# Encoder convolution net on two images: the order in which the level 1 matmul groups of the two images are issued

## The chip, the cores and the metric
One core of one Trainium2 chip runs the program once per launch. The metric is the device time of that launch in microseconds; the profile is of one such execution, and its times count from the first instruction of the span.

## The reference
`x` is (2 images, 32 channels, 64, 64), float32. Each channel is normalized over its plane, then a small U-shaped net runs, and its result is added to `x`. `BN_S` is a constant near 1.

```python
def basic_block(x, w1, w2, stride=1, ds=None):
    out = jax.nn.relu(conv3(x, w1, stride) * BN_S)
    out = conv3(out, w2, 1) * BN_S
    identity = conv1x1(x, ds, stride) * BN_S if ds is not None else x
    return jax.nn.relu(out + identity)
x = basic_block(x, e0b0c1, e0b0c2)
x = basic_block(x, e0b1c1, e0b1c2)
f0 = x
x = basic_block(x, e1b0c1, e1b0c2, stride=2, ds=e1b0ds)     # level 1
x = basic_block(x, e1b1c1, e1b1c2)
f1 = x
x = basic_block(x, e2b0c1, e2b0c2, stride=2, ds=e2b0ds)     # level 2
x = basic_block(x, e2b1c1, e2b1c2)
x = (jax.nn.relu(deconv2(x, dec0w) * BN_S) + f1) * BN_S
x = (jax.nn.relu(deconv2(x, dec1w) * BN_S) + f0) * BN_S
```

## The kernel before
Everything stays in SBUF between the input load and the output stores. A map is held as 2 x 2 pixel blocks: the 128 partitions are 4 pixel positions times 32 channels. A 3 x 3 convolution then is a few shifted matmuls from partitions to partitions.

Level 0 and level 1 work in "pieces": one image, a range of block rows, one PSUM bank. Level 1 has four stages, called here by their Python names: `down` (weights e1b0c1, stride 2), `block` (e1b0c2 and the shortcut e1b0ds), `odd` (e1b1c1) and `last_1` (e1b1c2). Each stage has two pieces per image, an upper and a lower one ("turned", its partition halves exchanged); such a pair goes together. The two pairs of a stage take four of the eight banks, so `down` and `odd` share banks 0 to 3, `block` and `last_1` share banks 4 to 7.

All matmuls of these pieces are 64 x 64 quarters of the array. Of a pair, the long products (`mains`: four shifts per piece, six in `down`) use one pairing of quarters and the short ones (`minors`: two shifts, three in `down`) the other, into the same bank; so `minors` first waits on the semaphore `mains_done` until the last of its pair's `mains` has ended. In the trace a float32 matmul shows as two records: `mains` of a pair are 32 records (48 in `down`), `minors` 16 (24 in `down`).

- `free_banks(pair)` makes TensorE (PE) wait until the pieces that held the pair's banks before are evacuated. For `down` and `block` these are the eight pieces of e0b1c2, the last stage of level 0: `down[0]` and `down[1]` wait for the four of image 0, `block[0]` for the first two of image 1 and `block[1]` for its last two.
- `mains` waits for its weights and for the pair's source: `down` for the stride planes `planes1` of its image (`wait_planes`; written by ACT L537 and L635 and by DVE L738 and L741 from `block0`, which DVE L791 adds up piece by piece), every other stage for both pieces of its image in the stage before.
- `shortcut_products(block[i])` (L1035, 16 records) reads `planes1` and starts the bank of `block[i]`; `identity_products(last_1[1])` (L1045, 8 records) reads `flat1` and starts the bank of `last_1[1]`. The `mains` of those pairs wait until they have ended.

The sums leave PSUM in the order of the pieces, which DVE and ACT have written out by hand: DVE takes both pieces of a `down` or `odd` pair (L783); of a `block` pair DVE takes the upper (L799) and ACT the lower (L558). Of `last_1`, image 0's two pieces go over DVE (L805 adds `flat1` to the sums), then DVE and ACT each make `planes2` of one (L748, L570) and gather `sides2` from it (DVE L758 in `gather(0)`, ACT L588 in `gather_sides(0)`). Image 1's follow behind that on both engines: DVE L748 and ACT L570 straight from PSUM, then sides and the corners (L762, L581).

Level 2 handles both images in one matmul. Its first stage, e2b0c1, runs `of_image(0)` (L1123, 4 records) once `planes2` of image 0 is there, then three whole products (L845, 6 records) after `even_planes` shows that both engines have made the first planes of both images, then `of_image(1)`, then the products of `sides2`. From there on each stage needs the whole result of the stage before.

ACT also rearranges the skip data of level 0 (L550, `gather_skip0`) between its level 1 evacuations, and GpSimd adds it up (L477).

Of the kernel before, what the change touches and what calls it, by code (L numbers as in the profile page):

```python
# [157 lines left out]
def previous_in_bank(piece):  # L158

    return max((p.index for p in PIECES[:piece.index] if bank_index(p.index) == bank_index(piece.index)), default=None)  # L160
# [21 lines left out]
def build(nc, x, consts, weights, out):  # L182
    ctx = ExitStack()
    with ctx:
# [3 lines left out]
        def sem(name):  # L188
            return ctx.enter_context(nc.semaphore(name))
# [26 lines left out]
        inside = [sb(f"inside{v}", [P, 1, SLOTS[v] * PITCH[v]]) for v in (0, 1)] + [sb("inside2", [P, IMAGES, RUN[2]])]  # L216
        zeros = sb("zeros", [P, BANK // 2], BF16)
        raw = sb("raw", [P, RAW_SLOTS, max(m for _, m, _ in WEIGHTS), P])
        w_sb = [sb(f"w_{n}", [P, 1, 9, P]) if n == "e1b0c1" else sb(f"w_{n}", [P, 1, m, P]) for n, m, _ in WEIGHTS]
        turned = {n: sb(f"turned_{n}", [P, 9 if n == "e1b0c1" else 4, P])  # L220
# [29 lines left out]
        mains_done = sem("mains_done")  # L250
# [24 lines left out]
        def wait_w(engine, k):  # L275

            if k == 0:
                engine.wait_ge(w_loaded[0], 16)
            else:
                engine.wait_ge(w_hi, k)  # L280
# [7 lines left out]
        def turned_rows(piece):  # L288

            return piece.row >= BLOCKS[STAGES[piece.stage].level] // 2  # L290
# [21 lines left out]
        def flat1_inside(piece):  # L312

            first = (piece.row + 1) * PITCH[1] + 1
            lines = flat1[:, piece.images[0], first:first + piece.rows * PITCH[1]]
            return lines.rearrange("p (r c) -> p r c", c=PITCH[1])[:, :, 0:BLOCKS[1]]
# [31 lines left out]
        def wait_evacuated(engine, index):  # L348

            wait_for(engine, index, evacuated_by)  # L350

        def of_stage(name, image):

            return [p for p in PIECES if p.stage == STAGE[name] and image in p.images]
# [9 lines left out]
        def sums_of(piece):  # L364

            stage, pitch = STAGES[piece.stage], PITCH[STAGES[piece.stage].level]
            if stage.level == 2:
                run = (EVEN_RUN if stage.kind == "even" else RUN)[2]
                return bank_of(piece)[:, 0:IMAGES * run].rearrange("p (i n) -> p i n", i=IMAGES)
            columns = BLOCKS[stage.level] if stage.kind == "even" else pitch  # L370
            return bank_of(piece)[:, 0:piece.rows * columns].rearrange("p (r c) -> p r c", c=columns)
# [45 lines left out]
        block = ctx.enter_context(nc.Block())  # L417
# [421 lines left out]
        def _(pe):  # L839
# [26 lines left out]
            def wait_source(piece):  # L866

                image, last = piece.images[0], last_row_read(piece)
                if piece.stage == 0:
                    pe.wait_ge(norm_by_dve, 2 * image + (1 if last < sum(NORM_BY_DVE[0]) else 2))  # L870
                    if last >= NORM_BY_ACT[0]:
                        pe.wait_ge(norm_by_act, image + 1)
                elif STAGES[piece.stage].kind == "down":
                    wait_planes(pe, 1, image)
                elif STAGES[piece.stage].level == 0:
                    wait_made(pe, last_piece(piece.stage - 1, piece.images, last))
                else:
                    for of_rows in [p for p in PIECES if p.stage == piece.stage - 1 and p.images[0] == image]:
                        wait_made(pe, of_rows.index)
# [97 lines left out]
            def mark(instruction):  # L977

                instruction.then_inc(mains_done, 1)
                marks[0] += 1  # L980
                return marks[0]

            def free_banks(pair):

                for piece in pair:
                    if previous_in_bank(piece) is not None:
                        wait_evacuated(pe, previous_in_bank(piece))

            def mains(pair, first=True, count=4, between=None):

                wait_w(pe, W_INDEX[STAGES[pair[0].stage].name])
                for piece in pair:
                    wait_source(piece)
                product = down_product if STAGES[pair[0].stage].kind == "down" else tile_product
                for n in range(count):
                    for piece in pair:
                        last = product(piece, True, n, first=(first and n == 0))
                    if n == 1 and between is not None:
                        between()
                return mark(last)  # L1000

            def minors(pair, done, count=2):

                pe.wait_ge(mains_done, done)
                product = down_product if STAGES[pair[0].stage].kind == "down" else tile_product
                for n in range(count):
                    for piece in pair:
                        last = product(piece, False, n, final=(n == count - 1))
                        if n == count - 1:
                            last.then_inc(summed, 1)  # L1010
# [12 lines left out]
            def shortcut_products(pair):  # L1023

                wait_w(pe, W_INDEX["e1b0ds"])
                for p in range(2):
                    for piece in pair:
                        h = int(turned_rows(piece))
                        first = (piece.row + 1 + 2 * h) * PITCH[1] + 1
                        of_h = slice(HALF * h, HALF * h + HALF)  # L1030
                        for c in range(2):
                            of_c = slice(HALF * c, HALF * c + HALF)
                            lines = planes1[of_h, piece.images[0], c, p, first:first + piece.rows * PITCH[1]].rearrange(
                                "p (r c) -> p r c", c=PITCH[1])[:, :, 0:BLOCKS[1]]
                            last = pe.matmul(sums_of(piece)[of_c], shortcut1[of_h, p], lines, start=(p == 0), stop=False,  # L1035
                                             skip_group_check=True)
                return mark(last)

            def identity_products(pair):

                pe.wait_ge(eye_loaded, 16)
                for piece in reversed(pair):
                    for c in range(2):
                        of_c = slice(HALF * c, HALF * c + HALF)
                        last = pe.matmul(sums_of(piece)[of_c], eye[of_c, of_c], flat1_inside(piece)[of_c], start=True,  # L1045
                                         stop=False, skip_group_check=True)
                return mark(last)
# [6 lines left out]
            for first in range(0, len(LEVEL0), GROUP):  # L1054
# [3 lines left out]
            pe.wait_ge(zeros_set, 6)  # L1058
            down, block, odd, last_1 = [[of_stage(name, image) for image in range(IMAGES)]
                                        for name in ("e1b0c1", "e1b0c2", "e1b1c1", "e1b1c2")]  # L1060
            free_banks(down[0])
            down_0 = mains(down[0], count=6)
            free_banks(block[0])
            shortcut_0 = shortcut_products(block[0])
            minors(down[0], down_0, count=3)
            free_banks(down[1])
            down_1 = mains(down[1], count=6)
            pe.wait_ge(mains_done, shortcut_0)
            block_0 = mains(block[0], first=False)
            minors(down[1], down_1, count=3)  # L1070
            free_banks(block[1])
            shortcut_1 = shortcut_products(block[1])
            minors(block[0], block_0)
            pe.wait_ge(mains_done, shortcut_1)
            block_1 = mains(block[1], first=False)
            free_banks(odd[0])
            odd_0 = mains(odd[0])
            minors(block[1], block_1)
            minors(odd[0], odd_0)
            free_banks(odd[1])  # L1080
            odd_1 = mains(odd[1])
            free_banks(last_1[0])
            last_0 = mains(last_1[0])
            minors(odd[1], odd_1)
            minors(last_1[0], last_0)
            free_banks(last_1[1])
            identity = identity_products(last_1[1])
            pe.wait_ge(mains_done, identity)
            minors(last_1[1], mains(last_1[1], first=False))

            def sums_2(name):

# [183 lines left out]
```

## Time and profile before

| | us |
|---|---|
| runs shown | 84.66, 85.80, 85.91 (median 85.8) |
| the profiled execution | 84.97 |
| its span, first to last instruction | 83.1 |
| level 1, first `down` matmul to first level 2 matmul | 51.99 to 67.77 |
| PE busy, share of the span | 74.2, 89% |
| DVE busy; ACT busy | 34.5; 43.1 |

A timeline row reads: start, length, engine, line, operation, output <- input, size, count; in brackets the idle time of the engine before it and what ended it. A merged row covers its count of instructions, in which the engine may have overlapped others; a matmul's shown length contains its way through the array, so groups of matmuls are measured from start to start.

### The profile page before, as it was taken

What the parts mean: (1) busy time and instruction counts of PE and PEld (TensorE: products, weight loads), DVE (VectorE), ACT (ScalarE), POOL (GpSimd) and SP (SyncE); (2) the same over time, 40 slices, a digit from 0 to 9 for tenths busy, and PEclk for the clock granted to TensorE, in tenths of its full rate; (3) what the DMA queues carried; (4) which work ended last, traced back from release to release, by engine and by line L of the source; (5) the groups of instructions that cost most, each with busy time, mean ns of one, the idle gap of its engine ahead of it and who ended that gap; (6) DMA issues with size and microseconds to landing.
All of it is one profiled execution on the core that took longest, in us unless ns stands there. A gap on an engine that the chain in (4) does not pass through costs nothing.

```text
span 83.1 us, 3230 instructions
## 1 busy us (share of the span) xinstructions
PE 74.2 (89%) x1395; PEld 60.9 (73%) x1395; DVE 34.5 (42%) x137; ACT 43.1 (52%) x113; POOL 8.5 (10%) x26
## 2 busy tenths in 40 slices
PE   4957799999999999999999999999999999799700
PEld 3735686777888887777788888999889878686500
DVE  5459829505736051070250742830412557113630
ACT  6006008980008999999757590997129367002300
POOL 7400000000000000000000009100650000000330
PEclk9999999999999999999999999999999999999999
DMA  1857990064000000409583000000000000000094
GB/s 13 237 167 197 326 351 10 0 166 122 8 0 8 0 0 8 130 10 317 179 270 114 8 0 0 8 0 8 0 8 0 8 0 0 0 0 0 8 323 182
DMA packets 4190, 6.62 MB, mean 80 GB/s; under 512 B 465, under 2 KB 2129, under 8 KB 4177
## 3 DMA queue, kind: packets, MB, share of 16 engines
q1 hardware_dynamic: 4032, 6.29, 23.8%
q8 instruction: 11, 0.18, 0.9%
q10 hardware_dynamic: 144, 0.13, 0.5%
q14 instruction: 3, 0.02, 0.1%
HBM read 5.37 MB, written 1.05 MB: 77 GB/s over the span
## 4 chain that ended last, share of the span: by engine, by line
PE 82%; DVE 6%; DMA 4%; issue 2%; SPq 1%; DVEq 0%
PE psum L955 63%; PE psum L845 7%; PE psum L970 6%; DMA x_sb<-x_in 4%; DVE late_a L834 2%; DVE late_b L701 1%; PE psum L1123 1%; PE psum L1035 1%; SPq L424 1%; PE psum L920 1%; PE psum L1170 1%; DVE stats L672 1%; DVE moments L685 1%; PE psum L913 1%; PE psum L887 1%
## 5 line engine op out<-in xcount | busy, mean ns | idle before, releaser
L955 PE MATMUL psum<-late_b,w_e0b0c 64*64 64x264 f32 (+1 forms) x192 | 11.5, 393 | 1.0 <-DVE late_b L701 1.0
L955 PE MATMUL psum<-late_b,w_e0b1c 64*64 64x264 f32 (+1 forms) x192 | 11.3, 391 | 0.0
L783 DVE SCALAR_TENSOR_TENSOR late_a<-psum,inside 128x297 f32<-128x297 f32 (+1 forms) x16 | 6.4, 444 | 11.8 <-PE psum L955 11.6
L955 PEld LDWEIGHTS psum<-late_b,w_e0b0c 64*64 64x64 f32 x192 | 8.2, 132 | 3.8 <-issue 1.5
L955 PE MATMUL psum<-late_a,w_e0b0c 64*64 64x256 f32 x96 | 10.6, 376 | 0.0
L955 PE MATMUL psum<-late_a,w_e0b1c 64*64 64x256 f32 x96 | 10.6, 375 | 0.0
L955 PE MATMUL psum<-late_a,turned_e0b0c 64*64 64x256 f32 x96 | 10.5, 375 | 0.0
L955 PE MATMUL psum<-late_a,turned_e0b1c 64*64 64x256 f32 x96 | 10.5, 375 | 0.0
L955 PEld LDWEIGHTS psum<-late_b,w_e0b1c 64*64 64x64 f32 x192 | 8.4, 132 | 2.7
L477 POOL TENSOR_TENSOR normed<-normed,x_sb 128x1024 f32<-128x1024 f32 x2 | 4.7, 2360 | 53.7 <-ACT normed L577 46.9
L955 PEld LDWEIGHTS psum<-late_a,w_e0b0c 64*64 64x64 f32 x96 | 7.7, 132 | 1.2
L955 PEld LDWEIGHTS psum<-late_a,w_e0b1c 64*64 64x64 f32 x96 | 7.7, 132 | 1.1
L955 PEld LDWEIGHTS psum<-late_a,turned_e0b1c 64*64 64x64 f32 x96 | 7.3, 132 | 0.5
L955 PEld LDWEIGHTS psum<-late_a,turned_e0b0c 64*64 64x64 f32 x96 | 7.3, 132 | 0.6
L904 PE MATMUL psum<-zeros 128*128 128x256 bf16 x37 | 6.5, 335 | 1.1 <-DVE eps L706 1.1
L621 ACT ACTIVATE late_b<-block 128x256 f32<-128x256 f32 x8 | 2.8, 412 | 6.9 <-DVE block L788 6.8
L904 PEld LDWEIGHTS psum<-zeros 128*128 128x128 bf16 x37 | 4.3, 120 | 2.3 <-DVE eps L706 1.1
L791 DVE SCALAR_TENSOR_TENSOR block<-block,psum 128x256 f32<-128x256 f32 x8 | 3.0, 418 | 6.2 <-PE psum L955 6.0
L550 ACT ACTIVATE late_b<-normed 128x128 f32<-128x128 f32 x16 | 5.4, 434 | 0.0
L970 PE MATMUL psum<-planes,w_e1b0c 64*64 64x153 f32 x72 | 5.3, 289 | 0.0
L970 PE MATMUL psum<-planes,turned_e1b0c 64*64 64x153 f32 x72 | 5.2, 289 | 0.0
L595 ACT ACTIVATE scratch<-moments,eps 128x1 f32<-128x1 f32 x2 | 0.6, 295 | 8.7 <-DVE moments L685 8.7
(134 smaller groups left out, 131.9 us busy)
## 6 DMA issues: line engine op xcount, KB each, us to landing
x_sb<-x_in SPq DMA_DIRECT2D x4, 160.0 KB, 3.3
raw<-e0b1c_in SPq DMA_DIRECT2D x2, 256.0 KB, 4.2
raw<-e1b1c_in SPq DMA_DIRECT2D x2, 256.0 KB, 2.9
raw<-e2b1c_in SPq DMA_DIRECT2D x2, 256.0 KB, 2.8
raw<-e1b0c_in SPq DMA_DIRECT2D x1, 448.0 KB, 5.3
raw<-e2b0c_in SPq DMA_DIRECT2D x1, 448.0 KB, 3.2
x_sb<-x_in SPq DMA_DIRECT2D x2, 192.0 KB, 3.1
out<-late_a SPq DMA_DIRECT2D x1, 384.0 KB, 2.9
```

The source lines that it names most:

```text
L424: sp.dma_start(x_sb[:, image, row:row + rows, :], x[:, image, row:row + rows, :]).then_inc(x_loaded[image][n], 16)
L477: pool.tensor_tensor(normed[:, image], normed[:, image], x_sb[:, image], ALU.add).then_inc(skip0_added, 1)
L550: last = act.activation(target, source, ACT.Copy)
L621: act.activation(flat_inside(image, piece.row, piece.rows), block0_of(piece), ACT.Relu).then_inc(hi_ready, 1)
L672: last = dve.bn_stats(stats[:, image, STATS * n:STATS * (n + 1)], x_sb[:, image, row:row + rows, :])
L783: dve.scalar_tensor_tensor(out=odd_of(piece), in0=sums, scalar=0.0, in1=mask_of(piece), op0=ALU.max, op1=ALU.mult).then_inc(relu_ready, 1)
L791: dve.scalar_tensor_tensor(out=block0_of(piece), in0=block0_of(piece), scalar=0.0, in1=sums, op0=ALU.max, op1=ALU.add).then_inc(relu_ready, 1)
L834: dve.scalar_tensor_tensor(out=result[:, n], in0=last_bank(n), scalar=0.0, in1=skip0_of(n), op0=ALU.max, op1=ALU.add).then_inc(result_read ...
L845: last = pe.matmul(within(target, columns), w, within(moving, columns), start=(first and n == 0), stop=(final and n == len(terms) - 1), sk ...
L904: pe.matmul(psum[:, bank, 0:256], zeros[:, 0:P], zeros[:, 0:256], start=True, stop=True)
L955: last = pe.matmul(target, weights_of, moving, start=first, stop=final, skip_group_check=True)
L970: last = pe.matmul(bank_of(piece)[of_c, 0:count], w[of_h, 3 * s + t, HALF * o:HALF * o + HALF], planes1[of_h, piece.images[0], s % 2, t % ...
```

## The change
The calls at the head of `pe`'s level 1 are put in another order; no instruction of level 1 is added or dropped. Written as m (`mains`), n (`minors`), s (`shortcut_products`), i (`identity_products`), with the stage's letter (d, b, o, l) and the image:

```
before: d0m s0 d0n d1m b0m d1n s1 b0n b1m o0m b1n o0n o1m l0m o1n l0n i1 l1m l1n
after:  d0m s0 d1m d0n s1 d1n b0m b1m b0n b1n o0m o1m o0n o1n l0m i1 l1m l0n l1n
```

`free_banks` of `down[1]` and of `block[0]` stand ahead of everything. DVE's, ACT's and GpSimd's programs are the same.

```diff
-            free_banks(down[0])
+            for pair in down:
+                free_banks(pair)
+            free_banks(block[0])
             down_0 = mains(down[0], count=6)
-            free_banks(block[0])
             shortcut_0 = shortcut_products(block[0])
+            down_1 = mains(down[1], count=6)
             minors(down[0], down_0, count=3)
-            free_banks(down[1])
-            down_1 = mains(down[1], count=6)
+            free_banks(block[1])
+            shortcut_1 = shortcut_products(block[1])
+            minors(down[1], down_1, count=3)
             pe.wait_ge(mains_done, shortcut_0)
             block_0 = mains(block[0], first=False)
-            minors(down[1], down_1, count=3)
-            free_banks(block[1])
-            shortcut_1 = shortcut_products(block[1])
-            minors(block[0], block_0)
             pe.wait_ge(mains_done, shortcut_1)
             block_1 = mains(block[1], first=False)
-            free_banks(odd[0])
-            odd_0 = mains(odd[0])
+            minors(block[0], block_0)
             minors(block[1], block_1)
-            minors(odd[0], odd_0)
-            free_banks(odd[1])
-            odd_1 = mains(odd[1])
-            free_banks(last_1[0])
-            last_0 = mains(last_1[0])
-            minors(odd[1], odd_1)
-            minors(last_1[0], last_0)
-            free_banks(last_1[1])
-            identity = identity_products(last_1[1])
-            pe.wait_ge(mains_done, identity)
-            minors(last_1[1], mains(last_1[1], first=False))
+            for stage in (odd, last_1):
+                first = []
+                for pair in stage:
+                    free_banks(pair)
+                    added = identity_products(pair) if pair is last_1[1] else None
+                    if added is not None:
+                        pe.wait_ge(mains_done, added)
+                    first.append(mains(pair, first=added is None))
+                for pair, main in zip(stage, first):
+                    minors(pair, main)
```

## Rows read from the trace of the kernel before

**Rows 1.** The page's row of the granted TensorE clock in 40 slices.
```profile
PEclk9999999999999999999999999999999999999999
```

**Rows 2.** Chain that ended last, level 1: start, length, piece of work.
```profile
52.21 1.56 PE psum L970 x48
53.77 0.44 PE psum L1035 x16
...
57.42 0.78 PE psum L970 x24
```

**Rows 3.** Timeline of PE, level 1.
```profile
51.99 0.29 PE L970 MATMUL psum<-planes,turned_e1b0c 64*64 64x153 f32 x1
...
61.03 0.30 PE L955 MATMUL psum<-odd,turned_e1b0c 64*64 64x128 f32 x2
...
61.47 0.73 PE L955 MATMUL psum<-flat,w_e1b1c 64*64 64x153 f32 x16
62.42 1.22 PE L955 MATMUL psum<-flat,w_e1b1c 64*64 64x153 f32 x32 [0.22 <-issue]
63.42 0.30 PE L955 MATMUL psum<-odd,w_e1b1c 64*64 64x128 f32 x2
...
64.30 0.73 PE L955 MATMUL psum<-flat,w_e1b1c 64*64 64x153 f32 x16
64.82 0.30 PE L955 MATMUL psum<-odd,turned_e1b1c 64*64 64x128 f32 x2
...
65.26 0.64 PE L1045 MATMUL psum<-flat,eye 64*64 64x128 f32 x8
65.98 0.33 PE L955 MATMUL psum<-odd,w_e1b1c 64*64 64x128 f32 x2
...
67.17 0.33 PE L955 MATMUL psum<-odd,w_e1b1c 64*64 64x128 f32 x2
```

**Rows 4.** Timeline of DVE, end of level 0 to the start of level 2.
```profile
51.38 1.62 DVE L791 SCALAR_TENSOR_TENSOR block<-block,psum 128x256 f32<-128x256 f32 x4 [2.46 <-PE psum L955]
...
53.92 0.18 DVE L741 TENSOR_SCALAR planes<-block 128x32 f32<-128x32 f32 x1
...
58.24 0.54 DVE L783 SCALAR_TENSOR_TENSOR odd<-psum,inside 128x153 f32<-128x153 f32 x2 [2.68 <-PE psum L970]
...
61.72 0.29 DVE L799 TENSOR_SCALAR flat<-psum 128x128 f32<-128x128 f32 x1 [2.31 <-PE psum L955]
...
65.54 0.47 DVE L805 TENSOR_TENSOR with_identity<-flat,psum 128x128 f32<-128x128 f32 x2
...
66.57 0.62 DVE L758 COPY sides<-planes 32x82 f32<-32x82 f32 x3 [0.34 <-ACT planes L570]
```

**Rows 5.** Timeline of ACT, level 1 to level 2.
```profile
61.78 0.28 ACT L558 ACTIVATE flat<-psum 128x128 f32<-128x128 f32 x1 [2.33 <-PE psum L955]
...
66.05 0.42 ACT L570 ACTIVATE planes<-with_identity 128x64 f32<-128x64 f32 x2 [1.38 <-DVE with_identity L805]
66.56 0.83 ACT L588 ACTIVATE sides<-planes 64x82 f32<-64x82 f32 x3
67.93 0.34 ACT L570 ACTIVATE planes<-psum 128x64 f32<-128x64 f32 x2 [0.54 <-PE psum L955]
```

**Rows 6.** Timeline of PE's weight loads (PEld), which start a group after a wait.
```profile
59.11 0.17 PEld L955 LDWEIGHTS psum<-odd,w_e1b0c 64*64 64x64 f32 x2 [0.28 <-issue]
...
67.77 0.52 PEld L1123 LDWEIGHTS psum<-planes,w_e2b0c 128*128 128x128 f32 x4 [0.17 <-issue]
68.21 0.79 PEld L845 LDWEIGHTS psum<-planes,w_e2b0c 128*128 128x128 f32 x6
```

**Rows 7.** Timeline of PE at the start of the kernel.
```profile
1.07 3.75 PE L904 MATMUL psum<-zeros 128*128 128x256 bf16 x18 [1.07 <-DVE eps L706]
5.77 0.41 PE L887 MATMUL psum<-stats,same_channel 32*128 32x18 f32 x8 [0.94 <-DVE stats L672]
6.12 1.70 PE L904 MATMUL psum<-zeros 128*128 128x256 bf16 x14
```

## The prediction
> **What bounds the kernel now.** I read the page first, then the chain that ended last, then the timelines of PE, DVE and ACT side by side from the end of level 0 to the first stage of level 2. PE is busy for 89% of the span and the granted clock is at full speed throughout [rows 1]; the chain through level 1 is almost all PE [rows 2]. So in level 1 the time is the length of PE's instruction list plus the gaps in it, and a new order of the same instructions can only win or lose gaps. Behind level 1 the bound changes: level 2 needs both images, and its stages hang on DVE and ACT in turn. So I need three things from the rows: how long each group takes start to start, how long PE must wait from the end of one pair's short products to the next stage's long ones of that image (the turn), and how much work of DVE and ACT is hidden today because image 0 is ahead.
>
> **Lengths of the groups.** d-mains 1.56, shortcuts 0.44, d-minors 0.78 us [rows 2]. o-mains 63.42 - 62.42 = 1.00; l-mains 64.30 - 63.42 = 0.88, and b-mains, of the same 32 records and size, 0.88 too; o-minors 64.82 - 64.30 = 0.52; b-minors 61.47 - 61.03 = 0.44, l-minors likewise; identity with the wait for its end 65.98 - 65.26 = 0.72 [rows 3].
>
> **The turn.** For `down` and `odd`, where DVE takes both pieces: b1m's weights start at 59.11 [rows 6], 0.33 behind DVE's end at 58.24 + 0.54 = 58.78 [rows 4], and its first matmul about 0.03 later, at 59.14. d1n, whose sums those are, was issued to 57.99: b1m comes after s1 (0.44) and b0n (0.44) and an idle time of 0.28 before 59.14 [rows 2, 6]. Turn: 59.14 - 57.99 = 1.15 us. For `block`, where DVE and ACT share: b1n was issued to 61.47, ACT ended at 61.78 + 0.28 = 62.06 [rows 5], o1m started at 62.42 [rows 3]. Turn: 0.95 us. Whatever PE has to do between the two counts as cover; the rest is a gap.
>
> **Gaps in level 1 before.** b1m 0.28 [rows 6]. o1m: cover o0n, 0.52 of 0.95, gap 0.43. l1m: 0.72 with the identity products, of which 8 records at 27 ns (0.44 over 16, rows 2 say) would be 0.22; the rest is the wait for them. l1n: it waits for its own long products with nothing between, 67.17 - 65.98 - 0.88 = 0.31 gap [rows 3].
>
> **Part 1, the head.** d0m starts at 51.99 now, right behind level 0 [rows 3]. In the new order PE first waits for `block[0]`'s banks, the first two of DVE's four evacuations that start at 51.38 and take 1.62 together [rows 4]; the second ends at about 51.38 + 0.81 = 52.19. With the 0.36 from a releaser's end to the first matmul (as at b1m and o1m) d0m starts at 52.5, a gap of 0.5. Queued behind it is all of level 1. Then d0m and s0 run to 54.5. d1m now follows at once and needs image 1's planes, which DVE finishes at 53.92 + 0.18 = 54.10 [rows 4]; plus 0.36 is 54.46. So the two new waits lie over each other: without the first the second would cost 0.46. Bounds for both: 0.4 to 0.6; I take 0.5. Moving `free_banks(down[1])` costs nothing, since its banks were emptied before 51.38; the cover that d0n gave d1m is what is gone.
>
> **Part 2, the middle.** d1m ends at 56.09 (54.53 + 1.56), d0n 56.87, s1 57.31, d1n 58.09. b0m needs 56.87 + 1.15 = 58.02: just covered, by 0.07. b0m to 58.97. b1m needs 58.09 + 1.15 = 59.24: gap 0.27, as before. b1m to 60.12, b0n 60.56, b1n 61.00. o0m needs 60.56 + 0.95 = 61.51: its only cover is b1n, **a new gap of 0.51**. o0m to 62.51, o1m 63.51 (covered by o0m; the old gap of 0.43 is gone), o0n 64.03, o1n 64.55. l0m needs 64.03 + 1.15 = 65.18: its only cover is o1n, **a new gap of 0.63**. l0m to 66.06, identity and its wait to 66.78 (as before, nothing between them), l1m to 67.66, l0n 68.10 and l1n from 68.10 (the old gap of 0.31 is covered by l0n). Against 67.17 that is +0.93. As a sum of gaps: 0.50 + 0.51 + 0.63 - 0.43 - 0.31 = +0.90, and 0.03 rounding.
>
> **Part 3, the passage to level 2.** Before, l0n was issued to 65.26, and i1, l1m and l1n hid image 0's evacuation; only image 1's stood behind l1n. Now l0n ends at 68.10, and both engines do image 0's share in front of image 1's. L805 started 0.28 after l0n [rows 3, 4] although DVE had L783 to do just ahead; 0.25 is the usual step (61.47 to 61.72). So L805 starts at 68.35. From the start of L805, ACT's L570 started 0.51 and its L588 ended at 66.56 + 0.83 = 67.39, that is 1.85 later [rows 4, 5]; DVE's L758 ended at 67.19, 1.65 later [rows 4]. In the new order DVE is free for image 1 at 70.0 and ACT at 70.2. l1n's sums have been waiting there since 68.8. ACT's L570 for image 1 then starts at 70.25 in place of 67.93 [rows 5], 2.3 later. `even_planes` releases the three whole products (L845), which started loading at 68.21 [rows 6]: now at 70.5. `of_image(0)` takes 0.44 [rows 6] and runs from 69.6, in the shade. All that follows, sides, corners and the rest of level 2 and the decoder, hangs on the same two engines' image 1 work and moves by the same 2.3. Of that, 0.93 is PE's delay and 1.4 is image 0's evacuation, uncovered. Bounds of the second: nothing if DVE and ACT could have done image 0's share under l1n entirely (they can't: L805 alone needs l0n, which ends 0.44 before l1n does), and 1.85 - 0.44 + 0.3 = 1.7 if every wait falls on the bad side. GpSimd's second L477 and ACT's second `gather_skip0` move by 0.1 us with d1n and end near 64.3, long before L805 at 68.35: hidden.
>
> **Sum.** +0.93 + 1.37 = +2.3 us. Against the profiled execution: 84.97 + 2.3 = 87.3 (span 83.1 to 85.4). The median of the runs shown is 0.8 above that execution, by which it would be 88.1. The four times before lie at 84.7 and 85.0 or at 85.8 and 85.9, so I put the forecast between: 87.7.
>
> **A rule weighed.** New idle times of PE are 0.5, 0.5, 0.6 in level 1 and, from l1n's last matmul at 68.8 to 69.6, 0.8, then 0.4. At the start of the kernel PE was idle for 0.94 before 5.77, and the 14 warm-up matmuls right behind took 1.70 together, (1.70 - 0.33)/13 = 0.105 each, that is at full speed; the first 18 took 3.75, 0.20 each [rows 7]. So an idle time of that length left the clock up. The Trainium skill, "TensorE: Matmul & The Clock Gate", section "Why this matters for your kernels", warns that the array falls back to its lower clock when PE sits idle between bursts for too long. By it the new pauses could halve the clock of level 2, which is the third rival below; this trace gives it little weight.
>
> **Rivals.** (1) *Less is uncovered in the passage.* If image 1's work on DVE and ACT is not what level 2's start hangs on, or image 0's overlaps more of l1n, only PE's 0.93 and a part of the 1.4 remain: +0.9 to +1.6, 86.2 to 86.9 by the middle of the times. Against it: the chain in the code is serial on each engine. (2) *Faster: the pairs cover each other.* The two removed gaps (o1m, l1n) give 0.74, b1m's could go too. If the turn were no longer than the other image's short products, 0.44 to 0.52, the new gaps at o0m and l0m would vanish, and 84.6 would follow if also the passage were hidden by l1n. It decides at a turn of about 0.5; the rows show 0.95 and 1.15 for the very same instructions. (3) *The clock falls in level 2.* From 69.6 PE's share of the rest is some 8 us; at the warm-up's two rates, 0.20 to 0.105, that adds up to 7 us: 95. (4) *Nothing changes*, because PE reorders or hid it: against it, groups start in the order of the code in every row.
>
> **How the numbers follow.** Forecast 75%, rival 1 15%, rival 2 3%, rival 3 3%, rival 4 4%. The forecast's own spread is the two clusters of times (+-0.6) with 0.4 of the sum. Range 86.5 to 88.9: it takes in the upper part of rival 1 and leaves out the others. A measurement of this kernel can tell about 2% from no change, 1.7 us; my 2.3 is 2.7%, not far above it. Slower by over 2%: 0.76; within: 0.20; faster: 0.04.
>
> **What would show it.** In the changed profile: d0m's first record near 52.5; L955 with idle times of about 0.5 before o0m and 0.6 before l0m, none before l1n; l1n from 68.1; DVE L805 at 68.3; ACT's L588 of image 0 ending near 70.2; L845 on planes at 70.5; the last stores 2.3 later. The prediction is wrong if L845 comes clearly before 70, if the turns are shorter than 0.95 when both images are in step, or if PEclk falls.

## The result

The changed kernel runs in 88.06 us (median of 4; 87.26 to 88.30) against 85.34 us (84.66 to 85.91) for the kernel before: ratio 1.035, 95% interval 1.029 to 1.041, slower by about 2.7 us at the medians. The times of either kernel lie in two groups (before: 84.66 and 84.89, or 85.80 and 85.91), the upper of which comes from the start of the kernel, as the next rows show. The changed kernel's profiled execution took 88.16 us, the span 86.3 us, 3.2 more than before. PE is busy for 77.0 us in place of 74.2, again 89% of the span.

Of these 3.2 us 0.74 are not of the change: they arise at the start, where both kernels are the same. The timeline of PE at the start of the changed kernel:

```profile
1.07 4.02 PE L904 MATMUL psum<-zeros 128*128 128x256 bf16 x18 [1.07 <-DVE eps L706]
5.47 0.63 PE L887 MATMUL psum<-stats,same_channel 32*128 32x18 f32 x8 [0.38 <-DVE stats L672]
6.03 3.17 PE L904 MATMUL psum<-zeros 128*128 128x256 bf16 x14
9.13 1.13 PE L955 MATMUL psum<-late_b,w_e0b0c 64*64 64x297 f32 x8
```

The 14 warm-up matmuls took 3.17 us; in the profile of before 1.70 [rows 7]. From start to start that is (3.17 - 0.42)/13 = 0.21 us each, with 0.42 the shown length of one, against 0.105 before: half the speed, 1.2 in place of 2.4 GHz. The clock records in the two traces agree: the granted clock is recorded at full speed from 9.99 us on in the changed kernel, from 4.42 us on before. Level 0 then starts 0.33 later (9.13; before it was 8.80, from the timeline) and needs 0.41 longer to its last matmul row, since 9.13 to 9.99 ran at half speed. To keep this out, I measure each profile from the last matmul row of level 0 (51.82 before, from the timeline; 52.56 in the changed kernel): level 1 and all behind it lost 3.2 - 0.74 = 2.5 us.

Timeline of the changed kernel, PE with its weight loads, end of level 0 to level 2:

```profile
52.56 0.39 PE L955 MATMUL psum<-late_a,w_e0b1c 64*64 64x256 f32 x2
53.55 0.17 PEld L970 LDWEIGHTS psum<-planes,w_e1b0c 64*64 64x64 f32 x2 [1.06 <-issue]
53.58 0.35 PE L970 MATMUL psum<-planes,w_e1b0c 64*64 64x153 f32 x2 [0.63 <-DVE block L791]
...
62.03 0.27 PE L955 MATMUL psum<-odd,w_e1b0c 64*64 64x128 f32 x2
62.61 0.36 PE L955 MATMUL psum<-flat,w_e1b1c 64*64 64x153 f32 x4 [0.31 <-ACT flat L558]
...
66.28 0.33 PE L955 MATMUL psum<-odd,w_e1b1c 64*64 64x128 f32 x2 [0.43 <-DVE odd L783]
...
67.18 0.63 PE L1045 MATMUL psum<-flat,eye 64*64 64x128 f32 x8
67.87 0.33 PE L955 MATMUL psum<-odd,w_e1b1c 64*64 64x128 f32 x2
...
69.23 0.27 PE L955 MATMUL psum<-odd,turned_e1b1c 64*64 64x128 f32 x1
...
69.57 0.28 PE L955 MATMUL psum<-odd,w_e1b1c 64*64 64x128 f32 x2
...
70.50 0.52 PEld L1120 LDWEIGHTS psum<-planes,w_e2b0c 128*128 128x128 f32 x4 [0.89 <-DVE planes L748]
71.47 0.67 PEld L845 LDWEIGHTS psum<-planes,w_e2b0c 128*128 128x128 f32 x5 [0.45 <-ACT planes L570]
```

Three waits are new: d0m at 53.58 waits for DVE's L791 (before it followed level 0 at once, [rows 3]); o0m at 62.61 waits for ACT's L558; l0m at 66.28 for DVE's L783. Behind l1n, which now follows l0n at once (from 69.23), level 2 waits twice, for L748 and for L570. The same stretch on DVE and ACT, to be held against [rows 4, 5]:

```profile
52.12 1.62 DVE L791 SCALAR_TENSOR_TENSOR block<-block,psum 128x256 f32<-128x256 f32 x4 [2.46 <-PE psum L955]
...
65.38 1.06 DVE L783 SCALAR_TENSOR_TENSOR odd<-psum,inside 128x153 f32<-128x153 f32 x4 [2.73 <-PE psum L955]
69.46 0.48 DVE L805 TENSOR_TENSOR with_identity<-flat,psum 128x128 f32<-128x128 f32 x2 [3.02 <-PE psum L955]
...
69.97 0.41 ACT L570 ACTIVATE planes<-with_identity 128x64 f32<-128x64 f32 x2 [4.67 <-DVE with_identity L805]
70.48 0.83 ACT L588 ACTIVATE sides<-planes 64x82 f32<-64x82 f32 x3
71.22 0.30 ACT L570 ACTIVATE planes<-psum 128x64 f32<-128x64 f32 x2
```

DVE sees the sums of both `odd` pairs as one run of four, and L805 starts 3.9 us later than before (69.46 against 65.54), ACT's second L570 3.3 us later (71.22 against 67.93), with the 0.74 of the start in both.

### The profile page after: what moved, and what is told of

It is laid out like the page before. It is cut to its first block, busy times and chain, and to the rows that moved or that the text cites. A ratio compares the mean times of both kernels' runs of the same rounds, so it can differ in the third digit from the quotient of the medians.

```text
span 86.3 us, 3230 instructions
## 1 busy us (share of the span) xinstructions
PE 77.0 (89%) x1395; PEld 61.2 (71%) x1395; DVE 34.5 (40%) x137; ACT 43.0 (50%) x113; POOL 8.6 (10%) x26
## 4 chain that ended last, share of the span: by engine, by line
PE 82%; DVE 6%; DMA 4%; issue 2%; ACT 2%; DVEq 0%; ACTq 0%
PE psum L955 60%; PE psum L845 7%; PE psum L970 6%; PE psum L904 4%; DMA x_sb<-x_in 4%; DVE late_a L834 2%; DVE stats L672 2%; PE psum L1035 1%; DVE odd L783 1%; ACT sides L588 1%; PE psum L920 1%; PE psum L887 1%; ACT planes L570 1%; PE psum L1167 1%; DVE with_identity L805 1%
## 5 line engine op out<-in xcount | busy, mean ns | idle before, releaser
L783 DVE SCALAR_TENSOR_TENSOR late_a<-psum,inside 128x297 f32<-128x297 f32 (+1 forms) x16 | 6.4, 445 | 11.7 <-PE psum L955 11.6
L955 PEld LDWEIGHTS psum<-late_b,w_e0b0c 64*64 64x64 f32 x192 | 7.6, 137 | 3.9 <-issue 1.1
L904 PE MATMUL psum<-zeros 128*128 128x256 bf16 x37 | 8.2, 399 | 1.1 <-DVE eps L706 1.1
L904 PEld LDWEIGHTS psum<-zeros 128*128 128x128 bf16 x37 | 5.0, 139 | 2.9 <-DVE eps L706 1.1
L791 DVE SCALAR_TENSOR_TENSOR block<-block,psum 128x256 f32<-128x256 f32 x8 | 3.0, 418 | 6.2 <-PE psum L955 6.0
L970 PEld LDWEIGHTS psum<-planes,w_e1b0c 64*64 64x64 f32 x72 | 4.7, 132 | 1.1 <-issue 1.1
```

What stands on the lines that cost most here:

```text
L783: dve.scalar_tensor_tensor(out=odd_of(piece), in0=sums, scalar=0.0, in1=mask_of(piece), op0=ALU.max, op1=ALU.mult).then_inc(relu_ready, 1)
L791: dve.scalar_tensor_tensor(out=block0_of(piece), in0=block0_of(piece), scalar=0.0, in1=sums, op0=ALU.max, op1=ALU.add).then_inc(relu_ready, 1)
L904: pe.matmul(psum[:, bank, 0:256], zeros[:, 0:P], zeros[:, 0:256], start=True, stop=True)
L955: last = pe.matmul(target, weights_of, moving, start=first, stop=final, skip_group_check=True)
L970: last = pe.matmul(bank_of(piece)[of_c, 0:count], w[of_h, 3 * s + t, HALF * o:HALF * o + HALF], planes1[of_h, piece.images[0], s % 2, t % ...
```

## The experiments

One number is read from each profile, called **D** here: the start of the weights of level 2's whole products (PEld L845 on `planes`) less the start of the last matmul row of level 0. It is free of what happens at the start, and behind it all twelve profiles take nearly the same time to the end of the span (14.8 to 15.1 us). The kernel before has 68.21 - 51.82 = 16.39; the changed one 71.47 - 52.56 = 18.91, which is +2.52. The table gives D less 16.39 and the measured ratio to the kernel before. D is read from one execution of each kernel; the intervals of the ratios are 0.4 to 0.8 us to either side, wider than most steps between neighbours, so the steps rest on D and the times only agree with them.

| kernel | D less 16.39, us | ratio, 95% interval |
|---|---|---|
| the change | +2.52 | 1.035 (1.029 to 1.041) |
| late_frees | +2.14 | 1.021 (1.014 to 1.029) |
| l0n_early | +2.28 | 1.023 (1.015 to 1.032) |
| both_parts | +1.65 | 1.014 (1.008 to 1.020) |
| after_single | +1.70 | 1.016 (1.010 to 1.022) |
| l0n_last | +1.43 | 1.019 (1.009 to 1.028) |
| early_frees | +0.85 | 1.010 (1.006 to 1.015) |
| single_waits | -0.39 | 0.998 (0.993 to 1.002) |
| fewer_waits | -0.45 | 0.995 (0.990 to 0.999) |
| early_identity | -0.46 | 0.992 (0.988 to 0.997) |
| warm_21 | -0.46 | 0.990 (0.984 to 0.995) |

### late_frees: the hoisted waits put back

```diff
-            for pair in down:
-                free_banks(pair)
-            free_banks(block[0])
+            free_banks(down[0])
             down_0 = mains(down[0], count=6)
+            free_banks(block[0])
             shortcut_0 = shortcut_products(block[0])
+            free_banks(down[1])
             down_1 = mains(down[1], count=6)
```

> The changed kernel, but the waits for free banks of block[0] and down[1] stand behind d0m again, as before the change. In the changed profile d0m starts 0.87 us behind level 0 (corrected for a start of the kernel that took 0.74 longer), where I had forecast 0.5. Theory: that whole gap comes from the hoisted waits (DVE's second evacuation, then a row of waits that PE passes one by one). Then d0m follows level 0 without a gap, and d1m waits for image 1's planes in its place, to about 2.5 us behind d0m's start in place of 2.0; L845 on planes comes 0.35 us earlier than in the changed kernel measured from level 0's end, and the time is +2.1 us against before (ratio 1.025) where the changed kernel has +2.5 in its profile. Rival: the gap is image 1's planes or something else at the head, and nothing moves (+2.5).

PE and its weight loads in this kernel:

```profile
51.81 0.39 PE L955 MATMUL psum<-late_a,w_e0b1c 64*64 64x256 f32 x2
51.99 0.29 PE L970 MATMUL psum<-planes,turned_e1b0c 64*64 64x153 f32 x1
...
54.42 0.17 PEld L970 LDWEIGHTS psum<-planes,w_e1b0c 64*64 64x64 f32 x2 [0.47 <-issue]
...
70.34 0.67 PEld L845 LDWEIGHTS psum<-planes,w_e2b0c 128*128 128x128 f32 x5 [0.45 <-ACT planes L570]
```

d0m follows level 0 at once, and d1m waits in its place, 0.47 on the weight loads, for image 1's planes. D falls by 0.38 (0.35 expected): the hoisted waits cost the change 0.38, not the whole 0.85 that d0m lost (53.58 - 52.56 = 1.02, where 51.99 - 51.82 = 0.17 before).

### early_frees: only the hoisted waits, in the kernel before

```diff
-            free_banks(down[0])
+            for pair in down:
+                free_banks(pair)
+            free_banks(block[0])
             down_0 = mains(down[0], count=6)
-            free_banks(block[0])
             shortcut_0 = shortcut_products(block[0])
             minors(down[0], down_0, count=3)
-            free_banks(down[1])
             down_1 = mains(down[1], count=6)
```

> The kernel before, and of the change only the waits for free banks of down[1] and block[0] ahead of d0m. Theory (the hoisted wait and the wait of d1m for image 1's planes lie over each other in the change, which is why late_frees gave back only 0.37): here d1m comes behind d0n and never waits for planes, so the whole delay of d0m, 0.9 to 1.0 us, goes to the end: ratio 1.011. Rival: a delay at the head costs 0.4 wherever it stands: ratio 1.004.

```profile
52.98 0.39 PE L955 MATMUL psum<-late_a,w_e0b1c 64*64 64x256 f32 x2
53.98 0.35 PE L970 MATMUL psum<-planes,w_e1b0c 64*64 64x153 f32 x2 [0.61 <-DVE block L791]
...
70.22 0.67 PEld L845 LDWEIGHTS psum<-planes,w_e2b0c 128*128 128x128 f32 x5
```

D is +0.85: here the whole delay of d0m (53.98 - 52.98 = 1.00, less 0.17) reaches the end. The same three lines cost 0.85 or 0.38, by what stands behind them; in the change they lie over the planes wait of d1m. I had said 0.9 to 1.0 and the ratio 1.011; measured 1.010.

### l0n_last and l0n_early: one pair of short products, moved both ways

In the kernel before, l0n behind l1m (l0n_last):

```diff
             minors(odd[1], odd_1)
-            minors(last_1[0], last_0)
             free_banks(last_1[1])
             identity = identity_products(last_1[1])
             pe.wait_ge(mains_done, identity)
-            minors(last_1[1], mains(last_1[1], first=False))
+            last_1_main = mains(last_1[1], first=False)
+            minors(last_1[0], last_0)
+            minors(last_1[1], last_1_main)
```

> The kernel before, with one pair of short products, l0n, moved behind l1m, as the change has it; all else as before. Theory: l1m starts as before, since it waits for DVE's evacuation of o1n anyhow, l1n starts only 0.13 later (its own gap of 0.31 is covered by l0n's 0.44), but image 0's evacuation begins 2.0 us later and stands in front of image 1's: L845 on planes at about 69.6 in place of 68.2, time +1.35 us (ratio 1.016), which is the part of the change's loss behind PE. Rival: the passage hangs on l1n only: +0.1 us (ratio 1.001).

In the changed kernel, l0n ahead of i1 and l1m again (l0n_early):

```diff
                     free_banks(pair)
+                    if pair is last_1[1]:
+                        minors(last_1[0], first[0])
                     added = identity_products(pair) if pair is last_1[1] else None
...
                 for pair, main in zip(stage, first):
-                    minors(pair, main)
+                    if pair is not last_1[0]:
+                        minors(pair, main)
```

> The changed kernel, with the one pair of short products l0n moved back ahead of i1 and l1m. Theory (image 0's evacuation of last_1, 1.8 us on ACT, stands uncovered behind l0n): PE itself loses 0.3 at l0n and 0.3 at l1n, which now wait for their own long products, but image 0's evacuation is over when l1n ends, so L845 on planes comes 0.6 us EARLIER than in the changed kernel, time about +1.8 us against before. Rival (level 2's start follows PE's last product, and the evacuation of image 0 is a side matter): 0.6 LATER, +3.1 us.

The passage in l0n_last, on PE, DVE, ACT and the weight loads:

```profile
51.49 0.39 PE L955 MATMUL psum<-late_a,w_e0b1c 64*64 64x256 f32 x2
...
67.29 0.48 DVE L805 TENSOR_TENSOR with_identity<-flat,psum 128x128 f32<-128x128 f32 x2 [1.95 <-PE psum L955]
...
68.31 0.83 ACT L588 ACTIVATE sides<-planes 64x82 f32<-64x82 f32 x3
69.06 0.30 ACT L570 ACTIVATE planes<-psum 128x64 f32<-128x64 f32 x2
...
69.31 0.67 PEld L845 LDWEIGHTS psum<-planes,w_e2b0c 128*128 128x128 f32 x5 [0.45 <-ACT planes L570]
```

One move of 16 records costs 1.43 us, where I had said 1.35: L805 starts 67.29 - 51.49 = 15.80 behind level 0, before it was 65.54 - 51.82 = 13.72, and ACT comes to image 1's L570 only after image 0's L588; L845 is released by it. The rival (+0.1) is out. The other way round, in the changed kernel:

```profile
52.33 0.39 PE L955 MATMUL psum<-late_a,w_e0b1c 64*64 64x256 f32 x2
...
67.27 0.46 PEld L955 LDWEIGHTS psum<-odd,w_e1b1c 64*64 64x64 f32 x3 [0.38 <-issue]
67.61 0.14 PEld L955 LDWEIGHTS psum<-odd,turned_e1b1c 64*64 64x64 f32 x2
...
70.56 0.52 PEld L1123 LDWEIGHTS psum<-planes,w_e2b0c 128*128 128x128 f32 x4 [0.17 <-issue]
71.00 0.67 PEld L845 LDWEIGHTS psum<-planes,w_e2b0c 128*128 128x128 f32 x5
```

L845 now loads with no wait for ACT behind `of_image(0)`: PE is the bound of the passage again. But D fell by 0.24 only, not by 0.6. Some 0.3 of the missing part stands in the rows: l0n's first two loads start at 67.27 and the next ones only near 67.6, where both_parts has the third 0.05 behind the first (66.14 and 66.09, from its timeline). The cause of this pause is open, and so is whether it is of this one execution: the kernel's other three times (86.74 to 87.03) don't decide it. The sign went against the rival (which had D rise), the size was off in this profile; both_parts has the same move without the pause.

### both_parts: do the two returns add up?

The edits of late_frees and of l0n_early together.

> The changed kernel with both partial returns at once: the waits for banks stand late (as in late_frees) and l0n stands ahead of i1 and l1m (as in l0n_early). Those two moved L845 on planes, counted from the last matmul of level 0, from 2.51 us behind the kernel before to 2.14 and to 2.27. Theory of separate causes: the parts add up, 2.14 - 0.24 = +1.9 us (ratio 1.022), and what is left is the turn gaps at o0m and l0m and the planes wait of d1m. Rival: both returns took away the same slack, and it stays at +2.1 to +2.3.

```profile
51.49 0.39 PE L955 MATMUL psum<-late_a,w_e0b1c 64*64 64x256 f32 x2
...
69.53 0.67 PEld L845 LDWEIGHTS psum<-planes,w_e2b0c 128*128 128x128 f32 x5
```

D is +1.65, better than the expected +1.9 by about the pause. Against late_frees (+2.14) moving l0n gives 0.49, near the 0.6 first expected. So head and passage are separate causes. What is left was not taken apart by a run of its own; read from the rows it is the planes wait of d1m (0.47), the gaps at o0m (0.51) and l0m (0.64), and l0n's wait for its own long products (0.38), less the gap at o1m that is gone (0.43): 1.57 of 1.65.

### single_waits, after_single: what is in a turn

```diff
-                for piece in pair:
+                for piece in (pair[:1] if STAGES[pair[0].stage].level == 1 else pair):
                     wait_source(piece)
```

This leaves out no work and no distinct condition: in level 1 both pieces of a pair wait for the same semaphores and values. In the kernel before:

> The kernel before; each level 1 group of long products waits for its source once, not once for each of its two pieces (the second wait is for the same values). Theory: PE passes the waits ahead of a group one after another, about 0.1 us for two of them, also when they are long satisfied, as soon as the first had to wait. Two waits less at b1m, o1m and l1m, which have a gap: the turns fall from 1.15 and 0.95 by 0.1 each, -0.3 us in all (ratio 0.996). Rival: satisfied waits cost nothing, the 0.33 from DVE's end to the first weight load is the path of the signal: 0.0 us, the turns stay.

In the changed kernel:

> The changed kernel, each level 1 group of long products waiting once for its source. Theory (the turn contains a row of waits that PE passes one by one, about 0.1 us for two): shorter gaps at the head (by 0.1), at b1m (0.2), o0m (0.15) and l0m (0.1 to 0.2), together -0.6 us, so +1.9 us against before. If only the wait of image 0's evacuation behind l0n set the end, nothing would move (+2.5). Expected of the gaps in the change: o0m 0.54 to 0.4, l0m 0.65 to 0.5.

The turn of `block` in single_waits, o1m's:

```profile
51.61 0.39 PE L955 MATMUL psum<-late_a,w_e0b1c 64*64 64x256 f32 x2
...
61.35 0.28 ACT L558 ACTIVATE flat<-psum 128x128 f32<-128x128 f32 x1 [2.10 <-PE psum L955]
...
61.81 0.50 PEld L955 LDWEIGHTS psum<-flat,w_e1b1c 64*64 64x64 f32 x16 [0.33 <-DVE flat L799]
...
67.61 0.67 PEld L845 LDWEIGHTS psum<-planes,w_e2b0c 128*128 128x128 f32 x5
```

From ACT's end at 61.63 to the loads it takes 0.18; in the kernel before it took 0.33 (62.06 to o1m's first matmul at 62.42, [rows 3, 5], less 0.03 from its load to it). So part of the turn is not the path of a signal but waits that are satisfied and still passed one by one. D fell by 0.39 where 0.3 was expected; the measured times (ratio 0.998, interval 0.993 to 1.002) are too coarse to show that by themselves. In the changed kernel, where more turns lie open, the times show it too (1.035 to 1.016), and the rows show it at the head:

```profile
51.52 0.39 PE L955 MATMUL psum<-late_a,w_e0b1c 64*64 64x256 f32 x2
52.30 0.35 PE L970 MATMUL psum<-planes,w_e1b0c 64*64 64x153 f32 x2 [0.39 <-ACT planes L635]
...
69.61 0.67 PEld L845 LDWEIGHTS psum<-planes,w_e2b0c 128*128 128x128 f32 x5 [0.45 <-ACT planes L570]
```

d0m starts 0.78 behind the last level 0 row, in place of 1.02 (I had expected 0.1 less, it was 0.24), and D falls by 0.82 where 0.6 was expected. By the timelines the gap at o0m went from 0.51 to 0.36, that at l0m from 0.64 to 0.42. A third of what the change lost is bought back with no move of work at all.

The waits themselves stand in the traces, as semaphore instructions on PE's queue between the end of DVE's second L791 and d0m's first load. L341 is the line of `wait_for`; first in the changed kernel, then in after_single:

```profile
L341 PEldq EVENT_SEMAPHORE  x5: 51/51/51, 52.9 to 53.5; - x5
...
L341 PEldq EVENT_SEMAPHORE  x3: 51/51/51, 51.9 to 52.2; - x3
```

With one wait for the weights in each (L280), six have become four, and d0m comes 0.24 earlier: about 0.12 us for each. The Trainium skill, "Perfetto Trace Analysis", section "Identifying Dependency Chains", says that an instruction that waits on several engines may have semaphore instructions placed ahead of it for the further conditions; the trace agrees, with six of them ahead of one group here.

### fewer_waits, early_identity, warm_21: towards a faster kernel

From single_waits on the kernel before. fewer_waits:

```diff
-                wait_w(pe, W_INDEX[STAGES[pair[0].stage].name])
+                if STAGES[pair[0].stage].level != 1 or pair[0].images[0] == 0:
+                    wait_w(pe, W_INDEX[STAGES[pair[0].stage].name])
...
             odd_0 = mains(odd[0])
+            free_banks(odd[1])
+            free_banks(last_1[0])
             minors(block[1], block_1)
             minors(odd[0], odd_0)
-            free_banks(odd[1])
             odd_1 = mains(odd[1])
-            free_banks(last_1[0])
+            free_banks(last_1[1])
             last_0 = mains(last_1[0])
             minors(odd[1], odd_1)
             minors(last_1[0], last_0)
-            free_banks(last_1[1])
```

> The kernel before with single waits for the source (that alone brought L845 on planes 0.39 us forward in the profile), and besides the waits for banks of odd[1], last_1[0] and last_1[1] ahead of the short products before them, and no second wait for weights that image 0's group has already waited for. Theory: a further 0.1 at b1m and 0.1 to 0.2 at o1m; l1m now starts when the identity products have ended and gains nothing: -0.6 us in all against before (ratio 0.993). Rival: what is left of the turn is the path of DVE's signal, and it stays at -0.39 (0.9955).

D is 67.74 - 51.80 = 15.94, -0.45: a further 0.06 only, not 0.2; here the rival was nearer. early_identity adds

```diff
+            identity = identity_products(last_1[1])
             minors(odd[1], odd_1)
             minors(last_1[0], last_0)
-            identity = identity_products(last_1[1])
```

> As fewer_waits, with the identity products i1 ahead of o1n in place of behind l0n, so that their end is not waited for. Theory: l1m is then bound by the turn of o1n alone, with only l0n (0.44) as cover, and o1n itself moves 0.22 back: l1m at 0.9 behind o1n's end, 0.1 to 0.2 earlier than in fewer_waits, -0.75 us against before (ratio 0.991). Rival: the turn is no shorter than 1.1, then l1m comes 0.1 later than in fewer_waits.

D is 68.48 - 52.55 = 15.93: the identity's end is no longer waited for, but the turn of o1n takes its place. Nothing gained, a miss. The ratio of 0.992 beside fewer_waits' 0.995 says no more, with these intervals. warm_21 adds

```diff
-WARM_UP = [18, 14]
+WARM_UP = [21, 14]
```

> early_identity with 21 warm-up matmuls on zeros ahead of the first statistics in place of 18 (outputs as before). The times of every kernel here fall in two groups some 1 us apart; in the profiles of the longer group the 14 warm-up matmuls behind the statistics took 3.17 us, in those of the shorter one 1.70. Theory: the clock rises late when PE sits idle in front of the statistics (0.4 to 0.9 us); 21 matmuls at 0.21 us end at about 5.5, fill that time, and more of the times fall into the lower group: median 84.3 against 84.9 for early_identity. Rival: when the clock rises is a matter of chance at the start, and the median stays within 0.2, or the 3 matmuls hold up the statistics and it rises.

```profile
1.07 4.66 PE L904 MATMUL psum<-zeros 128*128 128x256 bf16 x21 [1.07 <-DVE eps L706]
5.66 0.63 PE L887 MATMUL psum<-stats,same_channel 32*128 32x18 f32 x8
6.22 1.74 PE L904 MATMUL psum<-zeros 128*128 128x256 bf16 x14
```

PE no longer idles ahead of the statistics, and the 14 matmuls behind them ran at (1.74 - 0.33)/13 = 0.108 us each. But the mechanism was not the one expected: the clock is recorded at full speed from 6.34 us on, and the statistics matmuls still took 0.63, as in the changed kernel; in seven profiles with 18 matmuls it was up between 3.84 and 5.58. Its six times lie at 84.01 to 84.49 us (median 84.28); those of early_identity, twelve, spread from 84.00 to 85.54, six of them over 85. At a ratio of 0.990 (0.984 to 0.995) it is 1% faster than the kernel before; its interval overlaps those of fewer_waits and early_identity. Six times are few; that all fell in the lower group fits the theory and doesn't prove it.

## Why the prediction was right

The time of 88.06 lies in the range of 86.5 to 88.9, 0.36 above the forecast of 87.7, and the loss from level 1 on, 2.5 us in the profile, against the 2.3 that were summed. The mechanism of each part was as told, but the closeness of the total owes something to luck: PE's part was 0.34 larger than summed and the passage 0.12 smaller. Point by point:

- **The head: right in place, too small.** Forecast 0.5 before d0m; it was 0.85. The waiting for DVE's second evacuation was as summed: L791 at 52.12 + 0.81 = 52.93. What failed was the 0.36 "from a releaser's end to the first matmul", carried over from b1m and o1m: here it took 53.58 - 52.93 = 0.65, since six waits stand on PE's queue ahead of this group, where b1m in before has three (L341, 58.8 to 59.0), and after_single took 0.24 off by leaving out two repeated ones. That is 0.29 of the missing 0.35; the rest is rounding, for 52.19 + 0.36 is 52.55 and not 52.5. That the head and the planes wait of d1m lie over each other was right (forecast 0.46 for the second, 0.47 on the loads in late_frees). By these terms the hoisted waits alone would cost 0.50 - 0.46 = 0.04; late_frees has 0.38, because the head came out larger.
- **The middle: right.** o0m 62.61 less the start of b1n's last pair at 62.03 and 0.07 to its end (in before the next group starts that much behind such a row, 61.40 and 61.47 in the timeline): gap 0.51, as forecast. l0m at 66.28, DVE's two evacuations of o0n ending near 65.38 + 0.53 = 65.91: it waits for DVE as forecast, with a gap of 0.64 (forecast 0.63). l1n without a gap, as forecast. l1n's last row moved from 67.56 - 51.82 = 15.74 (timeline of before) to 69.57 - 52.56 = 17.01, by 1.27, where 0.93 was summed; the difference is the head's 0.35.
- **The passage: right, slightly too large.** 2.52 - 1.27 = 1.25 against the forecast 1.37. The forecast had ACT's image 1 share start 70.25 - 68.35 = 1.90 behind L805; it was 71.22 - 69.46 = 1.76. l0n_last shows it alone in the kernel before (+1.43), with +0.13 of PE expected in it.
- **The clock: right.** Pauses of 0.89 between weight loads in the passage didn't slow level 2: from L845's loads to the end of the span it is 86.3 - 71.47 = 14.8, before 83.1 - 68.21 = 14.9, and the granted clock is recorded at full speed to 85.09, when PE has long finished. Rival 3 is out. In before, the clock went up at 4.42 and stayed up over the idle time of 0.94 that followed, so the rows spoke against it. The Trainium skill, "TensorE: Matmul & The Clock Gate", section "Why this matters for your kernels", which the prediction stretched to its new pauses, warns of longer ones than any here; the trace agrees with it so far as it shows no fall behind the 0.89.
- **The start: half seen.** I took the two groups of times as a spread of +-0.6 without a cause, and put the forecast between them. The profile of after was of the upper group, as three of its four times may be: 87.97 to 88.30 against 87.26. Forecast for like against like is 85.0 + 2.3 = 87.3 and 85.8 + 2.3 = 88.1, both within 0.2 of what was measured.

## What to carry to other kernels

Two streams half a stage apart hide more than PE's turn from stage to stage: the one that is ahead also hides its evacuation at the end, where the two must meet. Before grouping like work of both streams, set the cover of each turn (the work between a producer's last product and its consumer) against the turn's length read from the trace, and see what stands last at the join. A wait that is hoisted to the head of a stage costs what is not covered by the next wait on the same path: 0.38 or 0.85 here for the same lines. And count the waits ahead of a group when you carry a turn from one place to another: that was the term that came out too small here.

## What the runs showed of the hardware that was not expected

Waits that are long satisfied are not free right behind one that had to wait: with the repeated waits on the same values left out, D fell by 0.39 us in the kernel before and by 0.82 in the changed one. Each further semaphore instruction on PE's queue ahead of d0m cost about 0.12 us.

And the start of the kernel makes the two groups of times. With otherwise equal code, the 14 warm-up matmuls behind the statistics took 1.70 us in seven profiles and 3.17 us in four, and level 0's last matmul row starts at 51.49 to 51.82 in the first and at 52.33 to 52.98 in the others. The length of PE's pause ahead of the statistics does not decide it: pauses of 0.36 (l0n_last) and 0.94 (before, [rows 7]) went with 1.70, pauses of 0.38 (the changed kernel) and 0.77 (early_frees) with 3.17. What does is open. The clock records in the traces go with the times: full speed from 3.84 to 5.58 us on in the seven, from 9.55 to 10.47 us on in the four. The page's row doesn't show this, since it stands at full speed also ahead of the first record; there the spacing of like matmuls tells the clock. The row of the changed kernel, whose clock was at half speed up to 9.99 us:

```profile
PEclk9999999999999999999999999999999999999997
```
